# The last two matmul groups of stage two change places in elements 1 to 7 of a LoRA feed-forward kernel

## What is computed

```python
y = einsum('bsi,boi->bso', x, cond_weight[ids])            # stage one
base_out = einsum('btd,od->bto', y, base_W) + base_b       # stage two
logits = einsum('btd,nd->btn', y, router_W) + router_b     # 15 routes
probs = softmax(logits); topk_p, topk_i = top_k(probs, 8)
w = sum of topk_p onto the 8 experts through expert_map
h = einsum('btd,erd->bter', y, A)                          # 8 experts, rank 16
lora = einsum('bter,eor->bto', h * w[..., None], B) * 2.0
out = x + base_out + lora
```

## Time and profile before

| what | us |
|---|---|
| median of 3 runs | 402.16 |
| lowest and highest run | 400.67, 402.24 |
| profiled execution, its own time | 401.29 |
| its span, first to last instruction | 399.5 |
| TensorE matmuls, busy | 394.5 |
| VectorE, busy | 301.1 |
| ScalarE, busy | 158.6 |

### The profile page before, as it was taken

How to read it: one execution, slowest core, us unless ns; L and a number is a source line. 1 busy time by engine, 2 the same in 40 slices (tenths; PEclk the granted TensorE clock), 3 DMA queues, 4 the chain that set the end, 5 groups by cost and what they waited for, 6 DMA issues and landing times.

```text
span 399.5 us, 5973 instructions
## 1 busy us (share of the span) xinstructions
PE 394.5 (99%) x2102; PEld 348.5 (87%) x2102; DVE 301.1 (75%) x554; ACT 158.6 (40%) x226; POOL 8.5 (2%) x22
## 2 busy tenths in 40 slices
PE   8999999999999999999999999999999999999996
PEld 7889888898888988889888888888888898888985
DVE  2867998798968984789657996589846798467763
ACT  3766444672156402554026620355304542144300
POOL 0002210000000000000000000000000000000000
PEclk9999999999999999999999999999999999999999
DMA  7999598830457305652076510775026830464002
GB/s 290 401 391 400 97 203 270 295 108 0 174 194 263 105 0 210 208 219 99 0 263 223 200 50 24 260 277 174 0 86 230 308 110 0 147 222 158 2 0 105
DMA packets 27133, 67.56 MB, mean 169 GB/s; under 512 B 3442, under 2 KB 14194, under 8 KB 26994
## 3 DMA queue, kind: packets, MB, share of 16 engines
q1 hardware_dynamic: 25106, 62.47, 44.3%
q0 software_dynamic: 1872, 3.90, 4.9%
q10 hardware_dynamic: 144, 1.05, 0.7%
HBM read 58.08 MB, written 8.39 MB: 166 GB/s over the span
## 4 chain that ended last, share of the span: by engine, by line
PE 97%; DMA 1%; SPq 0%; DVE 0%; issue 0%
PE y_ps L825 29%; PE y_ps L827 15%; PE pl_ps L849 7%; PE x_ps L863 6%; PE x_ps L864 6%; PE x_ps L862 6%; PE s_ps L863 6%; PE s_ps L862 6%; PE s_ps L864 6%; PE pl_ps L852 4%; PE s_ps L877 1%; PE s_ps L879 1%; PE s_ps L878 1%; DMA w_raw<-in_wT 1%; PE y_ps L838 1%; PE x_ps L879 0%
## 5 line engine op out<-in xcount | busy, mean ns | idle before, releaser
L825 PE MATMUL y_ps<-x_split,w_hi 128*128 128x512 f32 x504 | 176.0, 393 | 0.0
L827 PE MATMUL y_ps<-x_split,w_lo 128*128 128x256 f32 x504 | 141.3, 280 | 0.0
L825 PEld LDWEIGHTS y_ps<-x_split,w_hi 128*128 128x128 f32 x504 | 94.4, 187 | 21.7 <-issue 0.4
L827 PEld LDWEIGHTS y_ps<-x_split,w_lo 128*128 128x128 f32 x504 | 95.4, 189 | 0.3
L395 ACT CAST w_hi<-w_raw 128x1024 fp32r<-128x1024 f32 x58 | 60.8, 1050 | 77.3 <-DMA w_raw<-in_wT 77.2
L521 DVE TENSOR_TENSOR w_lo<-w_raw,w_hi 128x1024 fp32r<-128x1024 f32 x58 | 70.9, 1224 | 16.4 <-ACT w_hi L395 14.8
L387 ACT COPY y_sum<-y_ps 128x256 f32<-128x256 f32 x63 | 23.4, 372 | 56.8 <-PE y_ps L827 56.8
L539 DVE TENSOR_TENSOR y_sum<-y_ps,y_sum 128x256 f32<-128x256 f32 x63 | 26.4, 419 | 18.5 <-ACT y_sum L387 18.1
L849 PE MATMUL pl_ps<-pl_split,y_hi 128*128 128x480 f32 x128 | 33.0, 379 | 0.0
L862 PE MATMUL s_ps<-st_hi,y_hi 128*128 128x464 f32 x80 | 30.4, 380 | 0.0
L863 PE MATMUL s_ps<-st_lo,y_hi 128*128 128x464 f32 x80 | 29.9, 373 | 0.0
(11 more groups left out here) (114 smaller groups left out, 538.4 us busy)
## 6 DMA issues: line engine op xcount, KB each, us to landing
w_raw<-in_wT SPq DMA_DIRECT2D x60, 512.0 KB, 3.7
res<-in_x SPq DMA_DIRECT2D x16, 512.0 KB, 5.0
x_raw<-in_xT SPq DMA_DIRECT2D x14, 512.0 KB, 4.9
out<-res SPq DMA_DIRECT2D x13, 512.0 KB, 2.8
early_raw<-in_wT SPq DMA_DIRECT2D x4, 512.0 KB, 8.6
hi_raw<-in_base_t SPq DMA_DIRECT2D x2, 928.0 KB, 9.8
st_raw<-in_base_t SPq DMA_DIRECT2D x2, 928.0 KB, 11.4
st_raw<-in_base_t POOLq DMA_DIRECT2D x2, 928.0 KB, 9.6
```

What stands on the lines that cost most here:

```text
L825: nc.tensor.matmul(y_ps[:, c % 2, :], w_hi[:, s, k, :], x_split[:, k, :, :].rearrange("p s t -> p (s t)"), start=(k == 0), stop=False)
L827: mm = nc.tensor.matmul(y_ps[:, c % 2, 0:T], w_lo[:, s, k, :], x_split[:, k, 0, :], start=False, stop=(k == KC - 1))
```

## The change

In stage two of elements 1 to 7, `lora_b(1, x_ps, H1)` goes ahead of the last product, right behind the wait on `x_added`. The wait on `t_lo_done` follows it and stands directly ahead of the product. The signal `x_ps_done` is given by the product's last matmul instead of the low-rank part's.

```diff
@@ -937,10 +937,10 @@
                 lora_b(0, w_ps, H1).then_inc(w_ps_done, 1)
                 lora_b(0, z_ps, H2).then_inc(z_ps_done, 1)
                 lora_b(1, v_ps, H2, begins=True).then_inc(v_ps_done, 1)
+                pe.wait_ge(x_added, x_adds(b, 3))
+                lora_b(1, x_ps, H1)
                 pe.wait_ge(t_lo_done, 4)
-                pe.wait_ge(x_added, x_adds(b, 3))
-                product(x_ps, y_block(1, 1), T4, begins=False)
-                lora_b(1, x_ps, H1).then_inc(x_ps_done, 1)
+                product(x_ps, y_block(1, 1), T4, begins=False).then_inc(x_ps_done, 1)
```

## The result

The changed kernel takes 404.13 us, median of 5 runs (403.80 to 405.01), against 401.85 for the kernel before (5 runs, 400.67 to 402.24). The two medians lie 2.3 us apart. The recorded ratio of the two sets of runs, which is not that of the medians, is 1.0068 with a 95% interval of 1.0051 to 1.0084: 2.7 us slower, somewhere between 2.0 and 3.4. The prediction, 402.2 with a chance of 0.93 for no change, was wrong. The profiled execution of the changed kernel took 405.01 us around a span of 403.2.

What follows compares the result with a forecast made beforehand. TensorE's dense matmul stream was taken as the bound, its length set only by the matmuls' number and widths. The terms summed to 0.00, about 0.01 either way, giving 402.2 us at the median, range 400.5 to 403.5.

Steps and rivals of the forecast that it cites:

- The cost of the moved groups: End of stage two: low-rank matmuls and product change places, 3.21 us together before and after, cost 0.00.
- the new seam: Step from the x_ps low-rank group to the product, with a wait between: 0.23 us, no added cost.
- the exit to stage one: Step from the last product matmul to the next element's first matmul: 0.21 us.
- the addition: VectorE's last addition should start 0.41 to 0.42 us behind the last product matmul, where it was in time.
- both waits: TensorE's waits on x_added (3.7 us to spare) and t_lo_done (1.74 to spare, then 2.43): cost 0, gain 0.
- the tail: After the kernel's last product matmul, the addition and final store: cost 0.00 to 0.01 us.
- Rivals A and B: At the new seam: A, TensorE drains, 2.5 us, chance 0.02; B, weight load alone exposed, 1.3 us, chance 0.04.
- no new wait of TensorE: Sign expected in the changed kernel's timeline: TensorE waits nowhere that it did not wait before.
- The sum is 3.21 us either way: End of stage two: product 2.52 us plus low-rank matmuls 0.69 take the same time in either order.
- The seams are the same set as well: Steps between matmul groups at stage two's end, 0.23, 0.21 and 0.23 us, only change places; cost 0.00.
- Rival C: Stage one runs at another pace, differing by 0.41 us; 5 more elements at the slower pace give 404.2; chance 0.02.
- a span off by over 1 us with these steps unchanged would mean C: Sign for a changed pace of stage one: span differs though the steps at stage two's end are as forecast.

Runs made afterwards that it cites:

- e13: The kernel before with one extra 32-column matmul, result overwritten, at the end of element 0's stage two; ratio 0.9998 to the kernel before, 400.94 us.
- e5: The changed kernel with one extra 128-column matmul, result overwritten, at the start of stage one of elements 1 to 7; 404.08 us.
- e11: The kernel before with element 0's x_ps low-rank group moved behind the two v_ps products, so six 512-column matmuls end its stage two; 401.58 us.
- e10: The changed kernel with one extra 32-column matmul, result overwritten, at the start of stage one of elements 1 to 7; 401.73 us.
- e8: The kernel before with the second pair of chunk 0 in stage one of elements 1 to 7 issued 256 columns first; 404.51 us.
- e9: The changed kernel with three extra 512-column matmuls, results overwritten, at the start of stage one of elements 1 to 7; 405.86 us.

## Why the prediction was wrong

**What held.** The cost of the moved groups (3.20 for 3.21), the new seam (0.23), the exit to stage one (0.21), the addition (0.41 behind the last product matmul), both waits never binding, the tail: the last product matmul started at 399.60, the addition at 400.01 and the final store at 400.74, so 1.14 from matmul to store, against 397.01 - 395.86 = 1.15. Rivals A and B are out, since a drained seam would show 0.58 and an exposed load 0.4. So all that the prediction asked of the end of stage two came true, and the forecast was wrong all the same. Of its signs only "no new wait of TensorE" failed, by the 1.1 us in element 1 of one execution, which is not part of the loss.

**The step that failed** is the first of the sum: "The sum is 3.21 us either way. The seams are the same set as well", with its "Cost 0.00". The count stopped at the next element's first matmul. It rests on what the prediction says at its opening, that "only the number and widths of the matmuls set its length", and so took the steps behind the edit for constants of their widths. They are not: the same 64 pairs take 22.19 or 22.60 us by how TensorE comes to them. The term put at nothing is 6 x 0.41 = 2.5 us, of 2.7 measured (2.0 to 3.4).

**Rival C** was this case, and had a chance of 0.02. That its 404.2 stands so near the 404.13 measured is luck: it counted one element too few, 0.41, and started from a median of 402.16 that five runs put at 401.85. The rows for it were on the table: 22.60 against 22.19 for the same instructions in one profile. Two errors lowered it. The difference was put down to "the traffic beside it" without a test, and since the diff moves no traffic, C seemed to have no reason. And "5 more elements" was miscounted: elements 2 to 7 are six. What e13 shows to matter between elements 1 and 2 is the code ahead of them, `first_stage2` against `stage2`, which is what the diff changes for the rest. The line that was to decide C, "a span off by over 1 us with these steps unchanged would mean C, to be read from stage one's lengths", is what the profile showed.

**What stays open.** Why TensorE keeps to one rhythm or the other. The steps of a pair are shared between two weight loads of 0.19 us, 0.38 in sum, and a pair takes 0.347 to 0.353, so loads overlap one another in each pair (at 156.26 and 156.38 us in the kernel before, each 0.19 long); which of this gives the period of three pairs no row shows. Nor is there a rule here for which entry leads where: 0, 1 and 2 wide matmuls behind the product, a 128-column one, and a swapped pair gave the three-beat rhythm; 3 wide and a 32-column one gave the even one; and three or six wide behind element 0's products did not. Nor is it known which holds in mid-stage turn the rhythm over.

## What to carry to other kernels

In the dense stream of matmuls here the steps were not constants of their widths. Where a kernel has such a stream, cut the timeline at the stages and compare equal stages with one another, before and after. If equal stages already differ within one profile, find out what precedes each before predicting that a reorder is free. When a reorder costs time and no wait shows, look at the code behind it, and try a short extra matmul at the entry: if the stage then changes by far more than the matmul costs, that speaks for a rhythm. A try that changes nothing rules nothing out: e5 and e11 failed where e10 and e13 worked.

## What the runs showed of the hardware

- A stream of alternating 512 and 256-column matmuls, each with its own weight load, ran at 0.347 or at 0.353 us per pair, 2% apart, at a granted clock of 1.00 both times. In elements 2 to 7 of all 15 profiles each pace held from the entry to the end of the stage, 64 pairs in 8 chunks.
- Behind a hold in mid-stage one could turn into the other: 398, 391 and 398 ns in three stretches of one stage (e11), 398 and 391 in e8. In element 0 the rhythm differed between executions of identical code (399 and 394 ns).
- At the entry, one pair in the other order took the kernel before out of the even rhythm (e8), and one or three extra matmuls brought the changed kernel into it (e10, e9). A 32-column matmul, 0.11 us, saved 0.41.
- The mean recorded length of the 512-column matmuls tells the rhythms apart without any timeline: 391 to 394 ns at the even pace, 398 or 399 in the three-beat rhythm.
